# Layer 0's attention items: the result transposed in one pass, and the next item's rows requested ahead of a copy

## The reference, cut to what matters

```
q, k, v = heads(txt @ Wq), heads(image @ Wk), heads(image @ Wv)     # 16 heads of 64
dots = where(q_mask & kv_mask, q @ k.T * 64 ** -0.5, -max)
out  = softmax(dots) @ v
x    = x + tanh(g_xattn[0]) * (join_heads(out) @ Wout + bout)
```

## Time and profile before

| | us |
|---|---|
| Median of 3 runs | 618.66 (612.81 to 618.96) |
| The profiled execution, its own time | 618.59 |
| Its span in the trace | 616.9 |
| PE, DVE, ACT, POOL busy | 493.4, 383.3, 328.9, 219.4 |
| Mean granted clock of TensorE | 0.907 |

### The profile page before, as it was taken

How to read it: one execution, slowest core, us unless ns; L and a number is a source line. 1 busy time by engine, 2 the same in 40 slices (tenths; PEclk the granted TensorE clock), 3 DMA queues, 4 the chain that set the end, 5 groups by cost and what they waited for, 6 DMA issues and landing times.

```text
span 616.9 us, 16587 instructions
## 1 busy us (share of the span) xinstructions
PE 493.4 (80%) x5784; PEld 370.0 (60%) x5784; DVE 383.3 (62%) x1148; ACT 328.9 (53%) x953; POOL 219.4 (36%) x406
## 2 busy tenths in 40 slices
PE   3894988997889996899999999999999855029920
PEld 1631335655644544888888888888888733029920
DVE  0579965777346462678778787878787845204512
ACT  2563754554122212888787878787888713015410
POOL 9193942325100000444444444444434310530034
PEclk9996987999869996999999999999999988559975
DMA  8852644453099306000000699000000079330122
GB/s 321 289 204 102 217 141 114 131 145 102 6 341 351 111 1 273 3 2 3 3 0 0 204 314 290 6 3 2 2 0 0 2 288 428 135 99 15 27 61 68
DMA packets 47345, 74.08 MB, mean 120 GB/s; under 512 B 4428, under 2 KB 40828, under 8 KB 46140
## 3 DMA queue, kind: packets, MB, share of 16 engines
q1 hardware_dynamic: 42796, 60.51, 29.4%
q0 software_dynamic: 1472, 8.72, 3.9%
q10 hardware_dynamic: 3024, 4.13, 2.1%
HBM read 69.75 MB, written 3.60 MB: 119 GB/s over the span
## 4 chain that ended last, share of the span: by engine, by line
PE 52%; DVE 18%; ACT 12%; issue 7%; POOL 6%; DMA 3%; ACTq 1%; POOLq 1%; DVEq 0%; SPq 0%
PE ps L1555 10%; ACT work L829 7%; PE ps L1569 5%; PE ps L1489 5%; PE ps L1397 3%; PE ps L1681 3%; PE ps L1693 2%; PE ps L1505 2%; PE ps L1600 2%; DVE ps L1175 2%; POOL xe_scratch L716 2%; PE ps L1369 2%; POOL early_w L721 2%; DVE work L1209 2%; DVE sm L1186 2%
## 5 line engine op out<-in xcount | busy, mean ns | idle before, releaser
L829 ACT ACTIVATE work<-ps,nb,rkey 125x56 f32<-125x56 f32 x576 | 176.9, 404 | 50.5 <-DVE nb L1178 45.3
L1555 PE MATMUL ps<-work,region 128*64 128x96 f32 (+1 forms) x2304 | 117.0, 253 | 7.4 <-DVE work L1238 5.5
L1555 PEld LDWEIGHTS ps<-work,region 128*64 128x64 f32 (+1 forms) x2304 | 99.8, 137 | 19.2 <-issue 5.5
L687 POOL TENSOR_TENSOR work<-work,rs 125x336 f32<-125x336 f32 x96 | 72.1, 751 | 7.5
L1569 PE MATMUL ps<-region,work 125*64 125x129 f32 x1152 | 72.2, 273 | 3.1 <-POOL work L687 3.1
L1569 PEld LDWEIGHTS ps<-region,work 125*64 125x64 f32 x1152 | 64.0, 136 | 3.6 <-POOL work L687 3.6
L685 POOL TENSOR_TENSOR rs<-rs,rkey 125x6 f32<-125x6 f32 x96 | 19.4, 202 | 122.8 <-DVE rs L1190 122.8
L1175 DVE TENSOR_REDUCE ps<-ps 125x6 f32<-125x336 f32 x96 | 48.9, 509 | 17.9 <-PE ps L1555 17.5
L1186 DVE TENSOR_REDUCE sm<-work 125x6 f32<-125x336 f32 x96 | 47.4, 494 | 1.3 <-ACT work L829 0.7
L1397 PE MATMUL ps<-xln,folded 128*128 128x448 f32 x64 | 29.9, 591 | 10.3 <-ACT region L756 10.3
L954 DVE TENSOR_REDUCE sumsq<-region 125x12 f32<-125x1536 f32 (+1 forms) x16 | 27.7, 1746 | 8.0 <-ACT region L741 8.0
(11 more groups left out here) (294 smaller groups left out, 995.6 us busy)
## 6 DMA issues: line engine op xcount, KB each, us to landing
early_w<-in_ctx SPq DMA_DIRECT2D x16, 768.0 KB, 4.5
region<-in_ctx SPq DMA_DIRECT2D x16, 768.0 KB, 8.9
region<-in_w SPq DMA_DIRECT2D x6, 2048.0 KB, 19.7
region<-in_ctxT SPq DMA_DIRECT2D x16, 750.0 KB, 10.4
work<-in_ctxT_blk SPq DMA_DIRECT2D x22, 187.5 KB
early_w<-in_w POOLq DMA_DIRECT2D x1, 4096.0 KB, 12.4
region<-in_ctx_blk ACTq DMA_DIRECT2D x11, 192.0 KB, 2.6
early_w<-in_ctx_blk ACTq DMA_DIRECT2D x10, 192.0 KB, 2.6
```

The lines of the kernel that those rows point to most:

```text
L687: gp.tensor_tensor(shares_of(a, h), shares_of(a, h), bcast(rs[:, a, c], S), ALU.mult).then_inc(a_att, 1)
L829: i = act.activation(shares_of(a, h)[:, c, :], ps[:CP, 2 + 2 * a + h, c * S:(c + 1) * S], ACT.Exp, bias=nb[:, a, q:q + 1], scale=rkey[:, b ...
L1555: mm = pe.matmul(ps[r0:r1, 2 + 2 * a + h, c * S:c * S + WIDE], keysT[:, s, c0 + r0:c0 + r1], qT[:, p, a * S:a * S + WIDE], start=True, sto ...
```

## The change: the transposed result, and the place of a request

Two edits. In `transpose_result` on TensorE, the product of the result with the identity becomes an instruction of the transpose kind, as the transposes of the probabilities are already. It reads and writes the same tiles and raises the same semaphore.

On ScalarE, the wait on `o_mm` and `load_rows(j + 1, 1 - k)` move from behind the copy of the transposed probabilities to the head of an item's work, before the wait on `pt_mm`. An item's order on ScalarE is then: the request for the next item's rows, the copy, the exponential, the copy of the result. The condition for the request stays the same.

```diff
             with act.Fori(0, (n + 1) // 2) as i:
                 for k in range(2):
                     j = act.snap(i * 2 + k)
+                    act.wait_ge(o_mm, j + 2)
+                    load_rows(j + 1, 1 - k)
                     act.wait_ge(pt_mm, j + 1)
-                    act.wait_ge(o_mm, j + 2)
                     act.copy(PT[:KP].rearrange("p c r -> p (c r)"), ps[:KP, 2, 0:KC * 128]).then_inc(pt_ev, 1)
-                    load_rows(j + 1, 1 - k)
                     probabilities(j + AHEAD, k)
                     keep_result(j)
...
             def transpose_result(j):
                 pe.wait_ge(on_ok, j + 1)
                 pe.wait_ge(ot_ev, j + 1)
-                pe.matmul(ps[:, 4, 0:128], On, ident[:, :], start=True, stop=True).then_inc(ot_mm, 1)
+                pe.transpose(ps[:, 4, 0:128], On, ident[:, :]).then_inc(ot_mm, 1)
```

## The result

| | before | after |
|---|---|---|
| Median of 6 runs, us | 615.31 (612.81 to 618.96) | 626.94 (624.29 to 629.22) |
| Profiled execution, us | 618.59 | 628.55 |
| Its span, us | 616.9 | 626.8 |
| First scores (L1426) to first product with the folded output weights (L1469), us | 88.1 to 157.5 = 69.4 | 88.1 to 166.0 = 77.9 |

The changed kernel is slower: ratio 1.0184, 95% interval 1.0134 to 1.0234. Of the 10 us between the two profiled executions, 8.5 lie in the stage of the items.

The account below looks back on a forecast made before the run. The prediction took the circle by ScalarE's copy to bind, not TensorE. Its terms, +9.7 - 0.6 - 0.7 = +8.4 us on the profiled 618.59, gave 627.0 us; its own range was 625.4 to 629.7, for 8 in 10 620 to 632.

Parts of the forecast that it names:

- The circle by ScalarE's copy: Items' loop: value product, scores, exponential, copy of probabilities, next value product bind it; 5.75 us for two items.
- The price of the request: ScalarE's sequencer: register load, register work and DMA issue ahead of the copy count in full, 1.08 us.
- the two bounds: Request ahead of ScalarE's copy: 0.34 us if only the issue counts (rival, chance 0.13), 1.3 us with the loop's jump back.
- The rows, "worth nothing": Value product on TensorE: its waits for rows vanish, but lie beside the copy's circle, so they gain nothing.
- the rows' circle: Items' loop: second circle, by rows requested behind the copy, nearly as long; request to use 3.09 us.
- The length of the circle: Items' loop, two items: 5.75 us before, growing by 1.08 to 6.83 us after the move.
- nine copies at 1.08: ScalarE's copies of items 2, 4, ... 18: each delayed 1.08 us by the request, +9.7 us in all.
- The result in one pass: Result's transposition on TensorE: saving hidden from the third item on, counts in first two items and the last, -0.6 us.
- The end of the stage: VectorE's update at L1046: falls clear of POOL's last selects, which slow it; -0.7 us, bounds 0 and -0.7.
- Behind it everything only shifts: After the items' stage: everything starts from xT and is only shifted; the whole +8.4 us lies in the stage.
- The rival of the clock: TensorE, idle longer per item, returns to 1.2 GHz or rises late; 645 us if low throughout; chance 0.10, mostly for 629.
- late rise: TensorE's clock at the start of the items rises later than 98.8 us: 629 us, most of that rival's 0.10.

Follow-up runs that it names:

- m_only: Changed kernel with the one-pass transposition taken back, so only the request for rows moves ahead of the copy; 627.30 us, ratio 1.0174 to the kernel before.
- t_only: Kernel before with only the result's transposition made one pass, the request staying behind the copy; 617.43 us, ratio 1.0024 to the kernel before.
- keep_late: Kernel before with keep_result's load and copy moved behind the next item's copy of the probabilities; 614.94 us, ratio 0.9995 to the kernel before.
- rows_sp: Kernel before with the requests for rows moved from ScalarE's queue to SP's, result still in two passes; 625.25 us, ratio 1.0155 to the kernel before.

## Why the prediction was right, and where its sum was not

**The mechanism holds.** The circle by ScalarE's copy, and the request coming to lie on it, are what the runs show: m_only has the whole loss, t_only none, and the chain after has L784 and L785 between keep_result and C.

**The price of the request: right.** 1.08 us from the sequencer's rows before; 1.09 us from 121.80 to 122.89 after, and 6.63 - 5.52 = 1.11 us by the turns. Of the two bounds, the issue alone and the jump back added to it, neither came.

**The rows, "worth nothing": right in this profile.** The waits for rows lie beside the copy's circle but for one turn of six, and that one is 0.02 us longer than the undisturbed one. By t_only the rows' circle is only about 0.1 us longer than the copy's.

**The length of the circle: mis-sized.** The 5.75 us, and the turn of 5.78 whose legs the prediction adds up, are not the bare circle. The leg from S to E has 1.90 us there and 1.63 in the next turn; the rest is VectorE held up beside POOL. The prediction took VectorE's waits as going along unchanged, and priced such a delay only at the end of the stage, where it had a row for it. The bare circle is 5.52 us, and the move took away 0.19 us a turn of the delays: the net price of a turn is 1.11 - 0.19 = 0.92 us, not 1.08, and the turn is 6.63 us where 6.83 was forecast. So the term of nine copies at 1.08 is too large: with S at 88.1 in both, the V of item 18 comes at 156.75 instead of 148.31, +8.4 us, where +9.7 less 0.4 for the first two items was forecast.

**The result in one pass: right where it mattered.** It is hidden from the third item on (t_only's stage -0.4 us). The 0.6 us for the first and the last items is less than two traces differ by: the first V comes 0.3 us earlier than before in the changed kernel and 1.4 us later in t_only. The transposition does come to lie on the path in keep_late, which the prediction did not foresee.

**The end of the stage: wrong.** I expected 0.7 us back from POOL's selects. The update did get clear of them (0.22 us at 162.60), but the low clock ate it. The timeline of the changed kernel's last items:

```profile
156.75 1.65 PE L1451 MATMUL ps<-region,work 125*128 125x128 f32 x6 [1.47 <-ACT work L798]
...
158.83 1.46 PE L1426 MATMUL ps<-work 128*128 128x375 f32 x2
...
162.60 0.22 DVE L1046 SCALAR_TENSOR_TENSOR l_run<-l_run,early_w 128x1 f32<-128x1 f32 x1
```

V takes 1.65 us instead of 0.93 and the two passes of scores 1.46 instead of 0.80: the low clock, before the last items are done. From the V of item 18 to the first L1469 it is 9.3 us after and 9.2 before. So the 8.4 us of the sum and the 8.5 of the stage agree through two errors of about 0.9 us with opposite signs: 9.3 forecast and 8.4 measured up to that V, 0.9 less forecast and nothing measured behind it.

**"Behind it everything only shifts": not quite.** The products with the folded weights take 0.8 us longer (166.0 to 175.2 against 157.5 to 165.9), and up to the experts' first products another 1.0 us is added, most of it in the broadcast of the layer norm (L1369 on the chain 3.37 us against 2.43, at a granted clock of 0.50 from 182.3 to 186.4 us against 0.66 from 172.9 to 176.0). The rival of the clock came true at the very end of the stage and behind it, for about 1.8 us, besides the last items. Its late rise, 629 us, is a term that no run shows: at the start of the stage the clock is granted 0.51 up to 98.8 us in both kernels and 1.00 from there on.

**The time itself.** 627.0 forecast, 626.94 measured. The nearness is partly luck: six runs put the kernel before at 615.3 and not at the 618.7 of the first three, so the measured difference is 11.6 us (by the interval 8.2 to 14.4), and the profiled executions differ by 10.0, where 8.4 was forecast. What lies between is told above as far as one pair of traces can: 8.5 in the stage, 1.8 behind it. The rest of the medians' difference is open.

The page rule that I weighed, the Trainium skill, DMA: Bandwidth & Descriptors, section "Issuing engines are not separate DMA queues" (the sequencer's time to start a DMA is usually small beside the DMA itself), does not hold for this loop: the start with its register load is 1.09 us against a landing of 2.4, and rows_sp shows that a queue with three such starts an item is a bound by itself. The other, the Trainium skill, TensorE: Matmul & The Clock Gate, part 4 (the upper clock does not engage for transposes), did not show here: t_only ran at 0.99 with four transposes an item among its matmuls. No run here has transposes alone.

## What to carry to other kernels

A DMA request is work in its engine's queue; look for the stretch in which that engine waits for nothing but its turn, and keep the request out of it, even when the rows are needed sooner. Count a request with the register loads that make its address, in the row of the sequencer, and do the same for the queue that you want to move it to. If several circles of nearly one length lie side by side, look at each turn by itself before taking their mean as the length of one: here the shortest turn was the bare circle that the change acted on, and what lay above it in the others was an operation of another engine, which the change moved out of the way.

## What was not expected of the hardware

Some of VectorE's operations last until one of POOL's beside them ends: L1035 0.50 us instead of 0.22, ending at 128.20 us, where POOL's L637 ends at 128.19. Others don't: the maximum's second operation (L1037) takes 0.53 or 0.54 us with and without L637 beside it.

The granted clock fell to 1.2 GHz inside the stage when TensorE waited more per item: not at all before the last scores at a turn of 5.71 us, in the last items at 6.63 (in both kernels that have it), and in the midst of the stage at 7.18. rows_sp had nearly as long a turn as the changed kernel (6.52 us) and kept 1.00 from 102 to 145 us, as the changed kernel did, but its last two value products stayed short (0.93 and 0.83 us). What decides it was not tried.
